# A decoder, cross-attention and MXFP4 feed-forward kernel: the last bias enters the PSUM bank by a ScalarE copy in fp32 instead of a TensorE product of its bf16 split

## The reference

```
x = layernorm(x + decoder(x))                 # 4 layers, width 64: layernorm, silu, long convolution, MLP
x = layernorm(x + autocorrelation(x, ctx))    # per sequence of 64: circular correlation over time,
                                              # top 8 lags, softmax, weighted shifts of ctx
x = layernorm(x + quantize_mxfp4(x) @ quantize_mxfp4(weight).T + bias)
```

## Time and profile before

| | us |
|---|---|
| median of 3 runs | 324.72 (324.19 to 325.27) |
| the profiled execution | 324.38 |
| its span, first to last instruction | 322.2 |
| TensorE, VectorE, ScalarE, GpSimd busy | 269.6, 266.8, 239.5, 184.4 |

### The profile page before, as it was taken

The page is one execution under the profiler, slowest core; times in us unless marked ns, Lnnn a source line. Parts: engine busy times, 40 slices in busy tenths (PEclk is TensorE's granted clock), DMA queues, the critical chain, the costliest instruction groups (busy, mean ns, idle before and its releaser), DMA issues.

```text
span 322.2 us, 4490 instructions
## 1 busy us (share of the span) xinstructions
PE 269.6 (84%) x1088; PEld 110.6 (34%) x1096; DVE 266.8 (83%) x864; ACT 239.5 (74%) x556; POOL 184.4 (57%) x233
## 2 busy tenths in 40 slices
PE   1597788988989887898999999999989899769443
PEld 1223222322323232254543555534544434413110
DVE  5979989889889894458999999999999999876530
ACT  6056789889899798967767789888889785665524
POOL 1027422203204204023399989999999999997792
PEclk9999999999999999999999999999999999996955
DMA  6999999502114002500000000000000010000003
GB/s 208 395 263 341 344 164 219 141 2 63 39 29 132 31 0 40 92 2 1 2 0 1 2 0 2 33 35 35 3 33 34 33 35 34 1 33 35 33 34 130
DMA packets 14415, 24.56 MB, mean 76 GB/s; under 512 B 2611, under 2 KB 3251, under 8 KB 14390
## 3 DMA queue, kind: packets, MB, share of 16 engines
q1 hardware_dynamic: 12310, 20.09, 18.5%
q0 software_dynamic: 2080, 4.19, 7.6%
HBM read 15.89 MB, written 4.19 MB: 62 GB/s over the span
## 4 chain that ended last, share of the span: by engine, by line
POOL 35%; PE 21%; issue 13%; DVE 13%; ACT 13%; DMA 3%; SPq 1%; POOLq 0%; DVEq 0%; ACTq 0%
POOL big L893 5%; POOL big L886 5%; POOL big L899 5%; POOL xq L795 4%; POOL big L877 3%; POOL big L790 3%; POOL X L909 3%; DMA big<-in_xT_dram 3%; ACT L720 2%; PE ps L361 2%; POOL big L892 2%; PE ps L535 2%; PE ps L450 2%; PE ps L476 2%; PE ps L422 2%
## 5 line engine op out<-in xcount | busy, mean ns | idle before, releaser
L1074 DVE SCALAR_TENSOR_TENSOR X<-ps,X 128x512 f32<-128x512 f32 x48 | 31.2, 684 | 15.6 <-PE ps L504 6.6
L621 ACT ACTIVATE big<-X,lnv 128x512 f32<-128x512 f32 x48 | 34.3, 714 | 11.8 <-DVE X L1074 11.7
L372 PE MATMUL ps<-ctx_ring,consts 64*128 64x512 f32 (+1 forms) x96 | 34.9, 633 | 0.0
L422 PEld LDWEIGHTS ps<-consts,big 96*128 96x128 f32 x256 | 30.7, 192 | 6.6 <-DVE big L1109 2.7
L1151 DVE TENSOR_TENSOR big<-ps,ctxf 128x512 f32<-128x512 f32 x48 | 30.4, 681 | 1.9 <-PE ps L458 1.2
L422 PE MATMUL ps<-consts,big 96*128 96x64 f32 x256 | 30.9, 274 | 1.2 <-DVE big L1109 1.1
L649 ACT ACTIVATE X<-X,lnv 128x512 f32<-128x512 f32 x32 | 25.9, 809 | 0.6
L806 POOL TENSOR_TENSOR big<-big 128x512 f32<-128x512 f32 x4 | 5.8, 1443 | 35.4 <-DVE big L1187 25.2
L1139 DVE MATCH_REPLACE8 big<-w,big 128x64 f32<-128x64 f32 x128 | 25.1, 209 | 0.0
L886 POOL TENSOR_TENSOR big<-big 128x512 f32<-128x512 f32 x16 | 20.3, 1267 | 6.5 <-DVE big L1139 6.0
L790 POOL TENSOR_TENSOR big<-X,qs 128x512 f32<-128x512 f32 x20 | 20.9, 1048 | 1.6
(11 more groups left out here) (172 smaller groups left out, 664.5 us busy)
## 6 DMA issues: line engine op xcount, KB each, us to landing
big<-in_xT_dram SPq DMA_DIRECT2D x4, 1024.0 KB, 9.4
ctx_ring<-in_ctx_dram SPq DMA_DIRECT2D x16, 256.0 KB, 4.9
out_dram<-X SPq DMA_DIRECT2D x16, 256.0 KB, 2.0
X<-in_x_dram SPq DMA_DIRECT2D x2, 1536.0 KB, 11.6
X<-rows_sb POOLq DMA_DIRECT2D x1, 3072.0 KB, 21.6
X<-in_wq_dram SPq DMA_DIRECT2D x1, 1024.0 KB, 5.9
X<-in_x_dram SPq DMA_DIRECT2D x2, 512.0 KB, 4.1
X<-rows_sb POOLq DMA_DIRECT2D x1, 1024.0 KB, 8.7
```

The source lines that it names most:

```text
L372: mm(bank(LANE_BANK[lane]), mat((CY_0, CY_1, CY_C)[f])[half, :], ctx_ring[half, r * N:(r + 1) * N], start=True, stop=True).then_inc(s_cfor ...
L422: last = mm(ps[:, 2 * N + j * P + b * L:2 * N + j * P + (b + 1) * L], PQ[0:EVEN, b * N + j * P:b * N + (j + 1) * P], mat(IC_E)[0:EVEN, 0:L ...
L621: squared[k, n] = chain(a(JUNK[k], row(n), ACT.Square, bias=st[:, 0:1], scale=-float(V), accum_out=st[:, 2:3]))
L1074: stt(row(m), bank(b), 0.0, row(m), ALU.add, ALU.add, accum_out=st[:, 0:1]).then_inc(s_sum[k], 1)
```

## The change

The bias is copied, with its 128-row broadcast in SBUF as the source, by ScalarE into bank 1 (`bias_in`), and all four products are added onto it. TensorE's wait for `fed(n-1)` moves to ScalarE; TensorE waits for the copy (`s_bias`). On ScalarE the new step stands in round t behind `squares(0, t)` and ahead of `corr_out(t-3)`, for tile t-8. The split, its 3-row load, the block of ones and TensorE's L501 go; the broadcast of the second half of `rows` to 128 partitions (256 KB) is a new DMA beside the one of the first half, and GpSimd's `add_bout` waits for both.

```diff
@@ sync @@
-            sp.dma_start(rows_sb[0:SPLIT, V:2 * V], rows[V:2 * V].partition_broadcast(SPLIT)).then_inc(s_brow, 16)
...
-            sp.dma_start(rows_sb[:, 0:V], rows[0:V].partition_broadcast(P)).then_inc(s_rows, 16)
+            for k in range(2):
+                sp.dma_start(rows_sb[:, k * V:(k + 1) * V], rows[k * V:(k + 1) * V].partition_broadcast(P)
+                             ).then_inc(s_rows, 16)
@@ tensor: feed_forward(n) @@
                     if n == 0:
                         pe.wait_ge(s_qe[0], VC)
-                        pe.wait_ge(s_bias, 1)
-                    if n >= 1:
-                        pe.wait_ge(s_sum[2], n)
-                    mm(bank(1), ones[:, :], bias3[:, :], start=True, stop=False)
+                    pe.wait_ge(s_bias, n + 1)
                     pe.wait_ge(s_qe[1], n + 1)
                     for c in range(VC):
                         last = mm(bank(1), xqT[:, c * P:(c + 1) * P], wqT[:, c * V:(c + 1) * V],
-                                  start=False, stop=(c == VC - 1))
+                                  start=False, stop=(c == VC - 1), skip_group_check=True)
@@ scalar @@
+            def bias_in(n):
+
+                if here(n):
+                    if n == 0:
+                        act.wait_ge(s_rows, 32)
+                        act.wait_ge(s_hn, 2)
+                    else:
+                        act.wait_ge(s_sum[2], n)
+                    copy(bank(1), rows_sb[:, V:2 * V]).then_inc(s_bias, 1)
...
             for t in range(PAIRS + 10):
                 squares(0, t)
+                bias_in(t - 8)
                 corr_out(t - 3)
@@ gpsimd @@
-            g_.memset(ones[:, :], 1.0)
...
-                    pool.wait_ge(s_rows, 16)
+                    pool.wait_ge(s_rows, 32)
@@ vector @@
-            dve.wait_ge(s_brow, 16)
-            dve.wait_ge(s_mats, 16)
-            bias, b0, b1 = rows_sb[0:SPLIT, V:2 * V], part[:, 0:V], part[:, V:2 * V]
-            do(v_.tensor_copy(b0, bias))
-            do(tt(bias, bias, b0, ALU.subtract))
-            do(v_.tensor_copy(b1, bias))
-            do(tt(bias, bias, b1, ALU.subtract))
-            ch(ts(b0, b0, one_of(0), None, ALU.mult))
-            ch(ts(b1, b1, one_of(1), None, ALU.mult))
-            do(ts(bias, bias, one_of(2), None, ALU.mult))
-            do(tt(b0, b0, b1, ALU.add))
-
-            def bias_rows():
-                dve.wait_ge(s_winmm, 2)
-                tt(bias3[:, :], b0, bias, ALU.add).then_inc(s_bias, 1)
+            def identity_rounded():
+                dve.wait_ge(s_mats, 16)
                 v_.tensor_copy(ident_bf[:, :], mat(IDENT)).then_inc(s_idb, 1)
```

More of the change, by code:

```diff
@@ L178, in build @@
         woz = sb("woz", [P, 2 * V])
-        ones = sb("ones", [SPLIT, P], BF16)
         wqT = sb("wqT", [P, VC * V], BF16)
@@ L215, in build @@
         REST, G, PART, WN, WT = (piece(4 + k) for k in range(5))
-        part = ctxf[0:SPLIT, (3 * PAIRS - 2) * N:(3 * PAIRS - 1) * N].bitcast(BF16)
-        bias3 = win_sb[0:SPLIT, :].bitcast(BF16)
         PW = [piece(9 + k) for k in range(3)]
@@ L1016, in _ @@
             v_.tensor_copy(base[:, 0:1], bank(2)[:, DEPTH:DEPTH + 1]).then_inc(s_base, 1)
-            def one_of(k):
-                return mat(IDENT)[0:SPLIT, k:k + 1]
-            dve.wait_ge(s_brow, 16)
-            dve.wait_ge(s_mats, 16)
-            bias, b0, b1 = rows_sb[0:SPLIT, V:2 * V], part[:, 0:V], part[:, V:2 * V]
-            do(v_.tensor_copy(b0, bias))
-            do(tt(bias, bias, b0, ALU.subtract))
-            do(v_.tensor_copy(b1, bias))
-            do(tt(bias, bias, b1, ALU.subtract))
-            ch(ts(b0, b0, one_of(0), None, ALU.mult))
-            ch(ts(b1, b1, one_of(1), None, ALU.mult))
-            do(ts(bias, bias, one_of(2), None, ALU.mult))
-            do(tt(b0, b0, b1, ALU.add))
-            def bias_rows():
-                dve.wait_ge(s_winmm, 2)
-                tt(bias3[:, :], b0, bias, ALU.add).then_inc(s_bias, 1)
+            def identity_rounded():
+                dve.wait_ge(s_mats, 16)
                 v_.tensor_copy(ident_bf[:, :], mat(IDENT)).then_inc(s_idb, 1)
@@ L1192, in slot @@
                 if m == 0:
-                    bias_rows()
+                    identity_rounded()
                 elif first and s == 0:
```

## The result

The changed kernel takes 393.24 us (392.93 to 394.85), the kernel before 325.0 us beside it: ratio 1.211, 95% interval 1.207 to 1.216. I had forecast 367 us, with 346 to 380 as the range: slower as forecast, but by 68 us and not 42. The profiled execution took 392.93, its span is 390.9.

What follows compares the result with a forecast made beforehand. GpSimd bound the kernel before at 9.85 us a round; a TensorE-ScalarE loop of 12.87 us a full turn would replace it. 349.1 us at full clock plus 17.6 for clock falls gave 367 us, range 346 to 380.

Steps and rivals of the forecast that it cites:

- The bound, and the pairing of the two queues: TensorE starts feed_forward(7) some 2.7 us before ScalarE reaches the copy's place behind squares(0, 15); GpSimd then idles.
- What is removed: Sixteen L501 on TensorE, 0.31 us each, and the split on VectorE: their removal was held to be worth nothing.
- The start: On SyncE, without the 3-row load, x transposed loads up to 0.4 us sooner; tile 0's bias copy from 179.6 us.
- The copy: ScalarE's bias copy from SBUF to PSUM: 0.61 us, 0.66 with the semaphore, bounds 0.5 to 0.75.
- The loop at full clock: TensorE and ScalarE waiting in a circle: 12.87 us a full turn; alone, as a rival, 349 us, chance 0.27.
- The pause: TensorE's wait for ScalarE's bias copy before the next feed-forward product: about 3.5 us a turn.
- The clock: TensorE's clock falls to 1.2 GHz after pauses: 1.6 us a turn, 17.6 for tiles 0 to 10.
- the way to L695: Part of a turn, from L504's start on TensorE to L695's start on ScalarE: 4.17 us.
- L695 to L687: Part of a turn on ScalarE, with TensorE running L469, L396 and L438 between: 2.20 us.
- The rival with the low clock nearly throughout: Low clock in nearly all of TensorE's part of the turn: 381 us, 395 at the outermost, chance 0.10.
- The drain: From tile 11's bias copy through the last ScalarE rounds and the last tile to the span's end: 32.4 us.

Runs made afterwards that it cites:

- e3_place: The kernel before, with a one-column ScalarE copy at the place of bias_in and TensorE's L501 waiting for it; 393.4 us, ratio 1.207.
- e2_earlier: The changed kernel with the bias copy one place earlier in ScalarE's order, right behind squares(1, t-5); 326.11 us, ratio 0.999.
- e4_swap: The changed kernel with correlation and query_forms ahead of feed_forward on TensorE; 323.75 us, ratio 0.996.
- e11_no_bias: The kernel before without TensorE's L501, so the last bias is left out, the waits kept; 324.84 us, ratio 1.001.
- e12_fill1: The changed kernel with the last product of weight_forms issued one more time in TensorE's pause, from tile 3 on; 386.53 us, ratio 1.189.
- e5_fill3: The changed kernel with the last product of weight_forms issued three more times in TensorE's pause, from tile 3 on; 355.35 us, ratio 1.096.
- e6_front: The changed kernel with bias_in(t-8) ahead of squares(0, t) on ScalarE instead of behind it; 381.36 us, ratio 1.174.
- e1_fill: The changed kernel with the last product of weight_forms issued five more times in TensorE's pause, from tile 3 on; 369.15 us, ratio 1.132.

## Why the prediction was wrong, step by step

- **The bound, and the pairing of the two queues: right.** TensorE waits for the new copy, ScalarE for L420, GpSimd idles. e3_place shows that the place does it, e2_earlier and e4_swap that moving either end undoes it.
- **What is removed: nothing, right.** e11_no_bias for L501. VectorE's split had been in idle time: the instruction behind it starts at 21.44 us instead of 21.65.

```profile
21.44 0.75 DVE L1176 SCALAR_TENSOR_TENSOR big<-ps,base,big 128x512 f32<-128x512 f32 x1 [5.07 <-ACT big L717]
```

- **The start: 0.4 us forecast, none that can be told.** SyncE issues the loads of x transposed 0.4 us sooner, but TensorE's first product on them starts at 11.55 us, against 11.51 before. In e12_fill1, e4_swap, e5_fill3 and e6_front, whose first part is the same, it starts at 10.64, 10.82, 10.87 and 11.87, so one execution can't show a gain of 0.4. By 141 us the lead is 0.07 us. Then the clock fell once at 145 us, in work that is the same in both kernels:

```profile
144.00:146.00 2.00, 2.00 (x8) 0.73 0.02 4
146.00:148.00 2.00, 2.00 (x6) 0.50 0.00 0
```

That cost 0.9 us in this execution: a `normalise` that had been 0.07 us early before it came 0.84 us late behind it. The first copy came at 180.78, against 179.6 forecast: 1.2 us of the miss.
- **The copy: 0.61 us forecast, 0.58 measured.** This write into PSUM is a little faster than the writes into SBUF of 0.593 and 0.613, which goes the way of the Trainium skill's remark that ScalarE writes PSUM faster than SBUF ("ScalarE: Activation LUTs", Step-by-step: what each stage is for). But those two differ from it in source or function as well, and no run has the same copy into SBUF, so the remark is not shown by itself. In all it is 0.01 to 0.03 us, not the 0.11 between my 0.61 and the lower bound of 0.5.
- **The loop at full clock: right.** 12.69 measured, 12.87 forecast. From the first copy to tile 11's, e5_fill3 took 312.91 - 179.31 = 133.6 us, my terms 134.9. The pause was right too: 3.5 us forecast, 3.2 measured.
- **The clock: here the forecast failed.** That a pause of this length would let it fall was right; the size was not. The step is "I take 1.6, somewhat under the middle", between 0 and 4.17 us a turn. From the first copy to tile 11's the changed kernel took 357.22 - 180.78 = 176.4 us, so 42.8 more than e5_fill3, or 3.9 a turn. I had 17.6 for all eleven. Not one turn cost as little as 1.6: against e5_fill3's at the same place they cost 3.2, 4.3 to 4.4 five times, 3.9, 4.3, 2.8, 4.7 and 2.2. (Ahead of the products of tiles 10 and 11 e5_fill3's TensorE doesn't wait for the copy, so its extra products may lengthen its last two turns a little and make the clock's price look smaller.)
- **What misled me in it: three readings.** I let the one fall in the trace, which came 1 us after work resumed, stand for all; in the rounds of tiles 1 to 7 it came before the product. That one lasted 6.8 us; of the eleven here eight lasted 10.2, and only those of tiles 0, 8 and 10 lasted 6.8, in turns that cost 3.2, 2.8 and 2.2 us. And I counted only the way to L695: L695 to L687 hangs on TensorE too, and went from 2.20 to 3.00 us (239.05 to 242.05), while the way there went from 4.17 to 7.73. The two make 4.36 us, the 4.35 of a full turn, so 4.17 wasn't even an upper bound.
- **The rival with the low clock nearly throughout** was the case. I had given it 0.10 and 381 us, with 349.1 + 11 x 4.17 = 395 at the outermost. That 393 lies so near to 395 is luck in part: the clock cost 3.1 us less than 11 x 4.17 and the loop 1.3 less, the start and the drain 1.2 and 1.3 more.
- **The drain: 32.4 forecast, 33.7 measured** (390.9 - 357.22): 1.3 us.

The span was forecast at 364.5. 1.2 for the first copy, 176.4 - 134.9 - 17.6 = 23.9 for the turns and 1.3 for the drain make the 26.4 us by which it was longer.

## What to carry to other kernels

Before a wait is moved to another engine's queue, lay the two timelines over each other at one tile: when does this engine need it, when does that engine get to the place, and what does that engine need next from this one? If the answer closes a loop, its turn is a bound of its own, however idle the engines are; moving the step by one place at either end can undo it. And if TensorE is the one that waits, price all the TensorE work on the loop's path at half clock as a main case, not as an outlier: in full turns that was the price here.

## What the runs showed of the hardware

- A pause on TensorE costs more than its length. With 0.64 us left of it, the clock stayed at 1.00 (e5_fill3); with 2.36 us it fell in four turns of six (e12_fill1, tiles 1 to 6), with 2.42 in ten of eleven (e6_front, where the first is 2.77); with 3.2 us in all (the changed kernel). Even 1.56 us, in the three turns of e12_fill1 for tiles 8 to 10, was followed by a fall each time. In the eleven turns of the changed kernel the clock then stayed low for 6.8 or 10.2 us. Filling the pause with useless products took 38 us off the time.
- The fall can come inside the pause or over a microsecond after work has resumed, in turns of the same kernel, and shifts from turn to turn.
- Work that two kernels share can differ by a fall of the clock in one profiled execution, 0.9 us here: a difference of that size between two traces needs a second look before it is put down to an edit.
- Products of 64 rows that alternate between the two halves take 0.27 us an instruction (L458, four in the 1.07 us from its start to L501's), on one half alone 0.43 us (e1_fill, start to start).
